# Attention and routed FFN on one core: the next item's transposed scores ahead of the output projection, with other PSUM banks for the transposes

## The reference

```python
x = x + xattn(_layernorm(x), ctx)      # x, ctx: (128, 128, 256) f32, 16 heads of 16
x = x + ffn(_layernorm(x))
# xattn: q = ln(x) Wq', k = ctx Wk', v = ctx Wv'; softmax(q k' / 4) v per head, then Wo'
# ffn: 2 shared experts + top 4 of 16 routed experts (hidden 128),
#      gelu(x up') * gate, down'; the gate is the softmax probability of the router
```

## Time and profile before

| | |
|---|---|
| median of 3 runs | 2615.87 us |
| profiled execution | 2607.09 us, its span 2605.3 us |
| busy in the span | PE 2062.6 us (79%), PEld 1553.4, DVE 1587.6, ACT 1255.6, POOL 1218.3 |
| attention stage | to about 1475 us of the span |

### The profile page before, as it was taken

The page is one execution under the profiler, slowest core; times in us unless marked ns, Lnnn a source line. Parts: engine busy times, 40 slices in busy tenths (PEclk is TensorE's granted clock), DMA queues, the critical chain, the costliest instruction groups (busy, mean ns, idle before and its releaser), DMA issues. The chain is left out here.

```text
span 2605.3 us, 55887 instructions
## 1 busy us (share of the span) xinstructions
PE 2062.6 (79%) x20646; PEld 1553.4 (60%) x20646; DVE 1587.6 (61%) x4387; ACT 1255.6 (48%) x2364; POOL 1218.3 (47%) x1648
## 2 busy tenths in 40 slices
PE   5889898989889898888888789999999998970000
PEld 3656565656666666666565567787778777760000
DVE  3566666666666666665666346666666666654666
ACT  3454544454545455454544346666666666650000
POOL 1034444444434443434444637777777767770000
PEclk8999999999999999999999799999999999995555
DMA  8254545545454545453544467777777777759999
GB/s 263 82 162 145 175 151 164 165 149 175 147 172 146 172 143 175 142 175 126 170 139 160 175 219 242 255 240 247 259 259 242 256 260 241 262 194 373 411 413 358
DMA packets 373934, 547.32 MB, mean 210 GB/s; under 512 B 100385, under 2 KB 306210, under 8 KB 369570
## 3 DMA queue, kind: packets, MB, share of 16 engines
q1 hardware_dynamic: 321634, 393.20, 46.5%
q0 software_dynamic: 52032, 150.54, 15.3%
HBM read 241.12 MB, written 302.52 MB: 209 GB/s over the span
## 5 line engine op out<-in xcount | busy, mean ns | idle before, releaser
L1050 POOL DMA_INDIRECT xs<-xn,idx x512 | 503.3, 983 | 601.9 <-DVE xn L907 157.7
L1075 POOL DMA_INDIRECT yt<-yo,ix x572 | 552.9, 967 | 225.7 <-issue 144.0
L671 ACT ACTIVATE pr<-A 128x512 f32<-128x512 f32 x512 | 264.4, 602 | 396.8 <-PE A L505 396.8
L802 DVE TENSOR_REDUCE ms<-A 128x4 f32<-128x512 f32 x512 | 316.6, 680 | 75.4 <-PE A L481 74.4
L627 PE MATMUL A<-wt,hh 128*128 128x256 f32 x1144 | 244.2, 296 | 0.7 <-DVE hl L952 0.7
L941 DVE TENSOR_TENSOR xl<-A,xh 128x512 fp32r<-128x512 f32 x286 | 183.3, 681 | 100.7 <-ACT xh L722 100.5
L585 PE MATMUL A<-ident,xr 128*128 128x128 f32 x1400 | 187.6, 278 | 63.5 <-DMA xr<-xs 31.1
L585 PEld LDWEIGHTS A<-ident,xr 128*128 128x128 f32 x1400 | 161.2, 142 | 115.6 <-DMA xr<-xs 42.9
L540 PE MATMUL A<-wos,ot 128*128 128x256 f32 x512 | 164.9, 450 | 79.8 <-ACT ot L680 79.8
L501 PE MATMUL A<-qt,km 32*128 32x128 f32 x4096 | 219.7, 333 | 0.6 <-DVE mt L822 0.6
L501 PEld LDWEIGHTS A<-qt,km 32*128 32x128 f32 x4096 | 183.9, 211 | 54.1 <-issue 49.8
(11 more groups left out here) (145 smaller groups left out, 4098.9 us busy)
## 6 DMA issues: line engine op xcount, KB each, us to landing
xr<-xs SPq DMA_DIRECT2D x143, 576.0 KB, 5.1
xs<-empty SPq DMA_DIRECT2D x36, 2048.0 KB, 10.7
gb<-yt SPq DMA_DIRECT2D x32, 2048.0 KB, 16.1
xb<-in_x SPq DMA_DIRECT2D x32, 512.0 KB, 6.6
cg<-in_ctx_t SPq DMA_DIRECT2D x32, 512.0 KB, 4.0
yd<-xb SPq DMA_DIRECT2D x32, 512.0 KB, 3.2
x2d<-xn SPq DMA_DIRECT2D x32, 512.0 KB, 3.0
xr<-x2d SPq DMA_DIRECT2D x32, 512.0 KB, 4.6
```

The lines of the kernel that those rows point to most:

```text
L671: ac(pr[:, 4 * b:4 * b + 4, :].rearrange("p h s -> p (h s)"), banks[4 + b][:, :], ACT.Exp, scale=SCALE)\
L802: v.reduce_max(ms[n % 2][:, b, 0:4], banks[b][:, :].rearrange("p (h t) -> p h t", h=4), AX.X)\
L1050: q.indirect_dma_start(xs, bass.IndirectOffsetOnAxis(ap=idx[:, n, k:k + 1], axis=0), x2[g % 4][:, i, :], None).then_inc(sent[g % 4], 16)
L1075: q.indirect_dma_start(yt, bass.IndirectOffsetOnAxis(ap=ix[:, n % 8, k:k + 1], axis=0), yo[n % 4][:, k, :], None).then_inc(put[n % 4], 16)
```

## The change

The list of a slot becomes `first`, `S`, `PV`, `second`, `OTR`, `third`, `OT`, `MT`, `ST`, `OP`: the projection opens the slot, and ST stands ahead of OP. ST waits for `mt` only after the first four matmuls of its first round. OTR and OT use bank 0, MT and OP bank 3, in place of 7, 5 and 0; VectorE, ScalarE and the scatters' waits follow.

```diff
-ATT_BANKS = {... "PV": [5], "OTR": [7],
-             "MT": [5], "OT": [7], ... "OP": [0], "ST": [4, 5, 6, 7]}
+ATT_BANKS = {... "PV": [5], "OTR": [0],
+             "MT": [3], "OT": [0], ... "OP": [3], "ST": [4, 5, 6, 7]}
...
-        out += [("S", n + 1), ("SC", s), first, ("PV", n), ("SC", s + 1)]
+        out += [first, ("S", n + 1), ("SC", s), ("PV", n), ("SC", s + 1)]
...
-        out += [("SC", s + 2), third, ("OT", n), ("SC", s + 3), ("MT", n + 1), ("OP", n), ("ST", n + 1)]
+        out += [("SC", s + 2), third, ("OT", n), ("SC", s + 3), ("MT", n + 1), ("ST", n + 1), ("OP", n)]
...
             def MT(n):
                 pe.wait_ge(m_lo, n + 1)
-                wait_free(pe, 5, "MT", n)
-                tr(banks[5][:, 0:P], ms[n % 2][:, :, :].rearrange("p b k -> p (b k)"), ident[:, :])\
-                    .then_inc(fill[5], 1)
+                wait_free(pe, 3, "MT", n)
+                tr(banks[3][:, 0:P], ms[n % 2][:, :, :].rearrange("p b k -> p (b k)"), ident[:, :])\
+                    .then_inc(fill[3], 1)
 
             def ST(n):
                 g, i = divmod(n, GT)
-                wait_drained(pe, 5, "MT", n)
                 for b in range(4):
                     wait_free(pe, 4 + b, "ST", n)
                 for r in range(4):
...
+                    if r == 0:
+                        wait_drained(pe, 3, "MT", n)
                     for b in range(4):
                         rows = slice(32 * b, 32 * b + 32)
                         ins = mm(banks[4 + b][:, r * P:(r + 1) * P], sel[rows, r, :], mt[n % 2][rows, :], start=False, stop=True)
...
             def OP(n):
-                wait_drained(pe, 7, "OT", n)
-                wait_free(pe, 0, "OP", n)
+                wait_drained(pe, 0, "OT", n)
+                wait_free(pe, 3, "OP", n)
...
-                    b, stage, m = ((3, "S", at + 1), (5, "PV", at), (7, "OTR", at), (7, "OT", at))[k]
+                    b, stage, m = ((3, "S", at + 1), (5, "PV", at), (0, "OTR", at), (0, "OT", at))[k]
```

More of the change, by code:

```diff
@@ L36 @@
 AHEAD = 6
-ATT_BANKS = {"S": [0, 1, 2, 3], "K0": [4], "K1": [6], "Q0": [4], "Q1": [6], "VA": [4], "VB": [6], "PV": [5], "OTR": [7],
-             "MT": [5], "OT": [7], "XT": [1, 2], "XT2": [1, 2], "RL": [1], "RK": [1], "OP": [0], "ST": [4, 5, 6, 7]}
+ATT_BANKS = {"S": [0, 1, 2, 3], "K0": [4], "K1": [6], "Q0": [4], "Q1": [6], "VA": [4], "VB": [6], "PV": [5], "OTR": [0],
+             "MT": [3], "OT": [0], "XT": [1, 2], "XT2": [1, 2], "RL": [1], "RK": [1], "OP": [3], "ST": [4, 5, 6, 7]}
 FFN_BANKS = {"TR": lambda u: [0, 1], "U": lambda r: [2 + r % 2], "DN": lambda u: [4 + 2 * (u % 2), 5 + 2 * (u % 2)]}
@@ L523, in OTR @@
                 wait_drained(pe, 5, "PV", n)
-                wait_free(pe, 7, "OTR", n)
+                wait_free(pe, 0, "OTR", n)
                 for b in range(4):
-                    ins = tr(banks[7][:, b * P:(b + 1) * P], osb[:, b, :], ident[:, :])
-                ins.then_inc(fill[7], 1)
+                    ins = tr(banks[0][:, b * P:(b + 1) * P], osb[:, b, :], ident[:, :])
+                ins.then_inc(fill[0], 1)
             def OT(n):
-                wait_drained(pe, 7, "OTR", n)
+                wait_drained(pe, 0, "OTR", n)
                 flat = o[:, :, :].rearrange("p h d -> p (h d)")
                 for c in range(KC):
-                    ins = tr(banks[7][:, c * P:(c + 1) * P], flat[:, c * P:(c + 1) * P], ident[:, :])
-                ins.then_inc(fill[7], 1)
+                    ins = tr(banks[0][:, c * P:(c + 1) * P], flat[:, c * P:(c + 1) * P], ident[:, :])
+                ins.then_inc(fill[0], 1)
             def OP(n):
-                wait_drained(pe, 7, "OT", n)
-                wait_free(pe, 0, "OP", n)
+                wait_drained(pe, 0, "OT", n)
+                wait_free(pe, 3, "OP", n)
                 for c in range(KC):
-                    ins = mm(banks[0][:, 0:E], ot[:, c, :], wos[:, c, :], start=c == 0, stop=c == KC - 1)
-                ins.then_inc(fill[0], 1)
+                    ins = mm(banks[3][:, 0:E], ot[:, c, :], wos[:, c, :], start=c == 0, stop=c == KC - 1)
+                ins.then_inc(fill[3], 1)
             def XT2(g):
@@ L678, in OT @@
             def OT(n):
-                wait_filled(act_e, 7, "OT", n)
-                ac(ot[:, :, :].rearrange("p c s -> p (c s)"), banks[7][:, 0:E], ACT.Copy).then_inc(drain[7], 1)
+                wait_filled(act_e, 0, "OT", n)
+                ac(ot[:, :, :].rearrange("p c s -> p (c s)"), banks[0][:, 0:E], ACT.Copy).then_inc(drain[0], 1)
             def R1(g):
@@ L812, in OTR @@
             def OTR(n):
-                wait_filled(dve, 7, "OTR", n)
-                src = banks[7][:, :].rearrange("p (h w) -> p h w", h=NH)
+                wait_filled(dve, 0, "OTR", n)
+                src = banks[0][:, :].rearrange("p (h w) -> p h w", h=NH)
                 v.reciprocal(rd[:, :], src[:, :, HD]).then_inc(rd_ready, 1)
@@ L817, in OTR @@
                 v.tensor_tensor(o[:, :, :], src[:, :, 0:HD], rd[:, :].unsqueeze(2).broadcast_to([P, NH, HD]), ALU.mult)\
-                    .then_inc(drain[7], 1)
+                    .then_inc(drain[0], 1)
             def MT(n):
-                wait_filled(dve, 5, "MT", n)
-                v.tensor_copy(mt[n % 2][:, :], banks[5][:, 0:P]).then_inc(drain[5], 1)
+                wait_filled(dve, 3, "MT", n)
+                v.tensor_copy(mt[n % 2][:, :], banks[3][:, 0:P]).then_inc(drain[3], 1)
             def OP(n):
                 g, i = divmod(n, GT)
-                wait_filled(dve, 0, "OP", n)
-                v.tensor_tensor(xb[g % 4][:, i, :], banks[0][:, 0:E], xb[g % 4][:, i, :], ALU.add).then_inc(drain[0], 1)
-                wait_drained(dve, 0, "OP", n)
+                wait_filled(dve, 3, "OP", n)
+                v.tensor_tensor(xb[g % 4][:, i, :], banks[3][:, 0:E], xb[g % 4][:, i, :], ALU.add).then_inc(drain[3], 1)
+                wait_drained(dve, 3, "OP", n)
                 v.bn_stats(st2[:, i, :], xb[g % 4][:, i, :]).then_inc(y_ready, 1)
```

## The result

The changed kernel is slower: 2639.98 us, median of 4 runs (2623.69 to 2645.22), against 2614.92 for the one before in the same rounds; the ratio is 1.010, with a 95% interval of 1.0071 to 1.0129. The forecast was 2609, the other way. The profiled execution took 2623.69 us, the shortest of the four, with a span of 2622.0.

The account below looks back on a forecast made before the run. The load chain through `x2d`, `empty` and `xb` was to bound groups at 43.0 us, plus 1.36 for the low clock: 44.35 against 44.34, so 0 over 27 groups; with -7 at the ends, 2609 us, range 2575 to 2645.

Parts of the forecast that it names:

- OP's wait goes, 2.44 us a group.: TensorE's idle time for `ot` before the output projection, 0.86 in slots 1 and 3, 0.36 in 0 and 2, disappears.
- A wait for `mt` of 0.07.: ST's selectors start 0.66 us after MT, of which other matmuls cover 0.59: 0.07 a slot, bounds 0 and 0.60.
- VectorE takes the slots over.: With OP behind ST, TensorE waits for `o` ahead of OT in all four slots: about 2.0, 1.2, 1.0, 0.7 us.
- The chain through `x2d`, `empty` and `xb` sets the period.: `xb`'s load, queued behind the `x2d` store and clearing, takes 15.4 us and lands after LN1 asks in most groups.
- 43.0 us at full clock against 44.34.: A group's period in attention becomes 43.0 us (42.5 to 43.5), against 44.34 before with its low-clock time included.
- One low stretch in 0.85 of the groups, moved from slot 0 to slot 2, at 1.6 us.: TensorE's spell at the lower clock moves to slot 2, costing 1.36 us a group: 43.0 becomes 44.35.
- rival C: Second low-clock spell from slot 2's larger stall or slot 1: 2659 us in all groups, 2637 in half; chance 0.27.
- -7 at the ends.: Some five groups at the ends, without router work or without `xb`, save 1.4 us each, 7 us in all.
- The rule on transposes: Transposes do not count as busy for TensorE's clock, so slot 1, beside a stall of 1.2 us, could fall too.

Follow-up runs that it names:

- early load: Changed kernel with SP loading the next `xb` right after the store of `yd`, ahead of `x2d`, `empty` and `blank`: 2572.27 us, ratio 0.985; same edit in the kernel before: 2584.84 us.
- second execution: The changed kernel profiled once more without an edit: 2651.27 us.
- the filling: Changed kernel plus matmuls no one reads, ahead of OT in all slots and, in slot 2, ahead of OTR's wait and the router's logits: 2590.89 us, ratio 0.992.
- e2_st_ahead: Kernel before with the new banks and ST ahead of OP, but S still opening the slot: 2678.75 us, ratio 1.024.
- filling slot 0: Changed kernel with `xb` loaded right after the store of `yd`, plus 4 unread matmuls ahead of OT in slot 0 of the first 16 groups: 2575.21 us, ratio 0.986.

## Why the prediction was wrong

- **OP's wait goes, 2.44 us a group.** Right: 0.6 us are left in the kernel.
- **A wait for `mt` of 0.07.** Right: 0.66 from MT to the selectors, as summed.
- **VectorE takes the slots over.** Right: a wait for `o` in each slot, 1.97, 0.84, 0.65 and 0.65 where 2.0, 1.2, 1.0 and 0.7 were forecast. The chain from the maxima to OT with one copy in it was put at 4.02 and is 4.01 (721.98 to 725.99). Slot 1 was a little longer (11.78 for 11.45), slot 2 shorter where the load is in time.
- **The chain through `x2d`, `empty` and `xb` sets the period.** Half right. It lands 15.3 us after `x2d`, and LN1 waits in 20 groups; in the groups of 47.8 it doesn't wait, since the low clock makes them later than the load. The early load shows what it governs: 42.05 us a group without it, less the clock, against 42.55 with it.
- **43.0 us at full clock against 44.34.** The size was fair (42.55 measured), but what it was set against misleads: the kernel before less its own low stretches is at 42.74, below the 43.0. The change's gain in the chains is 0.2 us a group, 5 us in 27. The rest of the 2.44 came back in other waits, most of all for `o`.
- **One low stretch in 0.85 of the groups, moved from slot 0 to slot 2, at 1.6 us.** This is the step that failed, by its number: 1.36 us a group were put into the sum, and there were 43 stretches in 27 groups, 1.6 a group or 2.55 us, and 2.0 a group in the second execution. The price was right. The move to slot 2 was right too, for 23 of 31 falls, and from the 14th group on for all. Two things were missed. In the first 13 groups slot 0 fell as well, in eight of them, though OT came there 2.75 us after OTR (734.78 to 737.53) instead of 3.70, as forecast; the idle time right ahead of OT had stayed as it was, 1.97 for 1.96, and the prediction reckoned with the 3.7 and 2.7 only. And 12 falls lasted twice as long, for which it had no term. That is 16 more stretches than before at 1.6, or 26 us, against 5 won: 21, and 20.6 were measured in the 27 groups. The number is that of rival C, given 0.27, whose price for half of the groups was 2637. But C looked for a second fall from a larger stall in slot 2 or from slot 1; slot 1 never fell, and doubled falls, the larger part, were not in it. That its price fits is in part luck.
- **-7 at the ends.** Not seen apart. The profiled executions differ by 16.6 us, the 27 groups by 20.6, so 4 of these 7 us were won outside them.
- **The rule on transposes** (the Trainium skill, TensorE: Matmul & The Clock Gate, Part 4: PE-mode transpose). By it slot 1 could have fallen. In none of the 14 profiles of the table does a fall begin in slot 1 or slot 3, which have eight more transposes ahead of OT; all begin in slots 0 and 2. So nothing here bears the rule out, and nothing refutes it.

What is shown and what is not. That the low stretches make the difference is shown by their count in two executions of one kernel and by the filling (43 to 7, 1.8%). That the load has a part in them is shown by the early load (43 to 17). But its part is not simply that LN1 waits for a late `xb`: of the 16 stretches that the change added, 14 stand in the first 13 groups, where LN1 waits for 3.6 us in all. Why these groups keep four stretches in a row of groups until something shifts them, why falls come to last twice as long, and why the early load ends that too, stays open; so does whether ST behind a stall holds the clock down longer than OP did, which `e2_st_ahead` could not separate.

## What to carry to other kernels

Before costing a move on TensorE, write the period as full-clock time plus low stretches, for the kernel before as well: here the whole gain of a removed wait was 0.2 us a group, and the number of stretches, not their place, was worth five times that. When a wait goes, look at once for the transfer that was just in time (here a load behind 2 MB of clearing in the same queue, which landed some 15.4 us after the store ahead of it, where LN1 asked at 15.6 on average in the groups that didn't wait), and move its issue first: with the load early the same change turned from 1.0% slower to about 0.5% faster. Work that no one reads, put exactly into the waits that are left, can pay. Find first in which slot the clock falls: filling slot 0, which had the longest wait but few of the falls, won nothing.

## What was not expected of the hardware

- More matmuls made a kernel faster: 2591 us against 2640, with 7 low stretches against 43; but 2630 against 2616 where a load was due.
- The clock does not always fall at the longest wait: with the early load slot 0 mostly kept the full clock behind 1.96 us of idle time, and slot 2 fell behind 0.65 (14 falls of 17).
- The spread of one kernel on one core, 2624 to 2651 us, goes with the number of low stretches, 43 and 54 at the two ends, in an otherwise equal group of 42.55 us.
- The lower level stayed on with the engine busy under it, 4.00 of 4.00 us at 392 to 396, and in `e2_st_ahead` for up to 13.7 us at a time.
